# Order and queues of the first loads of a fused conditioning + low-rank FFN kernel, with a shorter warm-up and an earlier table load

## The reference, cut to what matters

```python
# x (64, 64, 1024) fp32; cond (64,) ints in 0..15; weights (16, 64, 64)
y = einsum('bct,bcd->bdt', x, weights[cond])          # conditioning, one 64x64 matrix per sample
yf = y.reshape(4096, 1024)
scores = yf @ Wr.T                                     # 64 experts
top_vals, top_idx = top_k(scores, 16)
G = zeros.at[rows, top_idx].set(softmax(top_vals))
h = einsum('nd,krd->nkr', yf, A)                       # A (64, 16, 1024): a 1024x1024 product
out = einsum('nkr,kdr->nd', h * G[:, :, None], B)      # B (64, 1024, 16): another one
return x + 2.0 * out
```

## Time and profile before

| | |
|---|---|
| runs (3) | 737.46 us median, 737.09 to 738.64 |
| the profiled execution | 737.22 us |
| its span, first to last instruction | 735.4 us |
| mean granted clock of PE | 0.995 of 2.4 GHz |
| PE busy | 716.5 us, 97% |
| PE weight loads busy | 600.9 us, 82% |
| DVE busy | 490.9 us, 67% |
| ACT busy | 262.8 us, 36% |
| POOL busy | 51.4 us, 7% |
| DMA | 178.41 MB, mean 243 GB/s |

### The profile page before, as it was taken

How to read it: one execution, slowest core, us unless ns; L and a number is a source line. 1 busy time by engine, 2 the same in 40 slices (tenths; PEclk the granted TensorE clock), 3 DMA queues, 4 the chain that set the end, 5 groups by cost and what they waited for, 6 DMA issues and landing times.

```text
span 735.4 us, 9259 instructions
## 1 busy us (share of the span) xinstructions
PE 716.5 (97%) x3440; PEld 600.9 (82%) x3440; DVE 490.9 (67%) x945; ACT 262.8 (36%) x498; POOL 51.4 (7%) x38
## 2 busy tenths in 40 slices
PE   8999989789999999999999999999999999999998
PEld 7878777578888888888888888888888888888886
DVE  4598899997433867965435469885544386887742
ACT  4567663332532642122222443312222264223100
POOL 0694700000000000000000000000000000000000
PEclk9999999899999999999999999999999999999999
DMA  9958349556986775566668586747577767544663
GB/s 321 408 202 289 121 166 404 210 209 261 310 309 227 285 261 203 210 215 235 238 245 289 200 324 236 246 162 270 199 256 256 270 249 290 185 170 175 228 227 143
DMA packets 56158, 178.41 MB, mean 243 GB/s; under 512 B 9650, under 2 KB 9778, under 8 KB 55602
## 3 DMA queue, kind: packets, MB, share of 16 engines
q1 hardware_dynamic: 53954, 172.78, 64.8%
q10 hardware_dynamic: 2160, 5.05, 1.9%
HBM read 131.66 MB, written 46.14 MB: 242 GB/s over the span
## 4 chain that ended last, share of the span: by engine, by line
PE 85%; DVE 13%; DMA 1%; issue 1%; ACT 0%; POOL 0%; DVEq 0%; POOLq 0%
PE Pb L265 38%; PE Pb L247 35%; PE Cb L227 6%; PE S L281 4%; DVE Cq L363 3%; DVE Wt L198 3%; DVE Op L180 2%; DMA xc<-in_x 1%; PE T L509 1%; DVE R L363 1%; DVE Xo L180 1%; DVE BR L363 1%; DVE xc L363 1%; DVE Q L363 1%; PE T L298 0%
## 5 line engine op out<-in xcount | busy, mean ns | idle before, releaser
L247 PE MATMUL Pb<-Op,Wt 128*128 128x512 f32 x1008 | 239.2, 393 | 6.4 <-DVE Op L180 4.6
L247 PEld LDWEIGHTS Pb<-Op,Wt 128*128 128x128 f32 x1008 | 187.4, 188 | 46.2 <-DVE Op L180 6.3
L265 PE MATMUL Pb<-Wt,Op 128*128 128x512 f32 x912 | 214.8, 394 | 7.0 <-DVE Op L180 7.0
L265 PEld LDWEIGHTS Pb<-Wt,Op 128*128 128x128 f32 x912 | 171.3, 190 | 43.5 <-DVE Op L180 8.7
L363 DVE TENSOR_TENSOR Q<-Pb,Q 128x512 f32<-128x512 f32 x112 | 77.4, 691 | 88.3 <-PE Pb L265 88.3
L265 PE MATMUL Pb<-Wt,Ox 128*128 128x512 f32 x432 | 100.8, 391 | 0.0
L265 PEld LDWEIGHTS Pb<-Wt,Ox 128*128 128x128 f32 x432 | 80.6, 188 | 16.3
L233 ACT COPY R<-Cb 128x512 f32<-128x512 f32 x60 | 35.2, 586 | 161.7 <-PE Cb L227 161.7
L180 DVE TENSOR_TENSOR Op<-R,Op 128x512 fp32r<-128x512 f32 x94 | 68.5, 753 | 28.8 <-ACT Op L178 28.8
L363 DVE TENSOR_TENSOR Cq<-Pb,Cq 128x512 f32<-128x512 f32 x64 | 44.0, 687 | 40.9 <-ACT Cq L374 30.9
L247 PE MATMUL Pb<-Ox,Wt 128*128 128x512 f32 x288 | 66.3, 390 | 0.0
(11 more groups left out here) (89 smaller groups left out, 486.9 us busy)
## 6 DMA issues: line engine op xcount, KB each, us to landing
Wt<-Wd SPq DMA_DIRECT2D x168, 512.0 KB, 4.9
Wd<-Wt SPq DMA_DIRECT2D x56, 512.0 KB, 4.2
Q<-in_x SPq DMA_DIRECT2D x32, 512.0 KB, 5.0
xc<-in_x SPq DMA_DIRECT2D x24, 512.0 KB, 4.0
out<-Q SPq DMA_DIRECT2D x32, 256.0 KB, 2.5
out<-Q SPq DMA_DIRECT2D x16, 512.0 KB, 2.8
BR<-in_x SPq DMA_DIRECT2D x12, 256.0 KB, 10.1
BR<-in_B SPq DMA_DIRECT2D x3, 1024.0 KB, 7.9
```

Source lines behind the costliest of these rows:

```text
L247: t = pe.run(lambda e, c=c, o=o, a=a, z=z: e.matmul(Pb[:, b, :], Wt[:, k, a, 128 * c:128 * c + 128], part(o, z), start=fresh and (c, a, z) ...
L265: t = pe.run(lambda e, c=c, o=o, k=k, a=a, z=z: e.matmul(Pb[:, b, :], part(o, a)[:, 128 * i:128 * i + 128], Wt[:, k, z, :], start=fresh an ...
```

## The change

- `WARM` goes from 24 to 14.
- The x blocks and A's half tiles that the first product uses are dealt to both queues: SP has x0, x1, x3 and A tiles 1 and 3; ACT has the table, x2, and A tiles 0 and 2. `Wr` and the identity come next on ACT, Wr now first.
- ACT does a 128x4 copy into `nm` behind its third issue, so that its table load stands there.
- A's tiles 4 to 7 move from the end of ACT's queue to the end of SP's.
- Unit 0 is split behind block 0, unit 1 behind block 2, unit 2 behind the first R copy; the second set of `wbd` copies (`cond_first(1)`) stands behind the R copies.
- The identity is awaited in `s_turn` and `g_turn` instead of before the loop.

```diff
-WARM = 24
+WARM = 14
@@ s_turn, g_turn
-            pe.after(tok, t_free[0])
+            pe.after(tok, t_free[0], t_id)
@@ the first loads
+        t_wa = ac.load(l_xc[0], lambda e: e.dma_start(Wa, wts))
         cn = sp.load(l_cn, lambda e: e.dma_start(cnd[:, :], cond.rearrange("(a b) -> a b", a=1)))
-        t_wa = ac.load(l_xc[0], lambda e: e.dma_start(Wa, wts))
-        for i in range(4):
-            load_x0(sp, i, 1)
-        for i in range(4):
-            load_an(ac, i, 1)
+        load_x0(sp, 0, 1)
+        load_x0(sp, 1, 1)
+        load_x0(ac, 2, 1)
+        load_x0(sp, 3, 1)
+        load_an(ac, 0, 1)
+        ac.after(z_s)
+        ac.run(lambda e: e.copy(nm[:, :], sS[:, 0:4]), False)
+        load_an(sp, 1, 1)
+        load_an(ac, 2, 1)
+        load_an(sp, 3, 1)
+        t_wr = ac.load(l_wr, lambda e: e.dma_start(SG[:, 0, :], Wr))
+        t_id = ac.load(l_id, lambda e: e.dma_start(idn[:, :], ident[:, :]))
         for i in range(4):
             load_x0(sp, i, 0)
-        t_id = ac.load(l_id, lambda e: e.dma_start(idn[:, :], ident[:, :]))
-        t_wr = ac.load(l_wr, lambda e: e.dma_start(SG[:, 0, :], Wr))
         for i in range(4):
             load_an(ac, i, 0)
         for a in range(2):
             for i in range(4, 8):
                 load_x0(sp, i, a)
         for j in range(4, 8):
-            load_an(ac, j, 0, 2)
+            load_an(sp, j, 0, 2)
@@ the four blocks
-            if i == 2:
-                a_unit(0, 0, an_ready[0][1])
+            if i == 0 or i == 2:
+                a_unit(0, i // 2, an_ready[i // 2][1])
         ops = [(op_spare.popleft(), parts[3]) for c in range(4)]
-        op_free[NO + 4] = cond_first(1)
         for i in range(4):
             ac.after(parts[i])
             R_ready[0][1] = ac.run(lambda e, i=i: e.copy(R[:, 0, 4:8, 128 * i:128 * i + 128],
                                                          banks[i].rearrange("p (c n) -> p c n", n=128)))
             (cb_free[0], cb_free[1], s_free, t_free)[i][0] = R_ready[0][1]
-            if i < 2:
-                a_unit(0, 1 + i, an_ready[1 + i][1])
+            if i == 0:
+                a_unit(0, 2, an_ready[2][1])
+        op_free[NO + 4] = cond_first(1)
         a_unit(0, 3, an_ready[3][1])
@@ before the main loop
-        pe.after(t_id)
```

## The result

Over 17 runs of each the changed kernel took 738.47 us (737.36 to 739.63), the kernel before 737.08 (735.89 to 738.83). The ratio is 1.0017, with a 95% interval of 1.0009 to 1.0024: **slower by 1.4 us**. That is just under the 1.5 us that the prediction took as the least that can be told from no change, but the interval leaves no change out. The forecast was 737.3, no change. The profiled executions stand at 738.47 and 737.22.

The account below looks back on a forecast made before the run. It took POOL's sums, in turns with VectorE, to set the T1 product, and PE to bound the next 22 us. 737.22 - 0.15 = 737.1, at the median's level 737.3; range 735.8 to 739.9.

Parts of the forecast that it names:

- The start: First product: would start at 13.0 instead of 14.79 us, a gain of 1.8 us there.
- Tile 4: Load of A's tile 4, at SP's end: lands at 24.3 to 25.3 us, 2.0 to 3.0 later than before.
- Gain at the T1 product: 0.15 us: Where PE resumes with T1: 54.3 instead of 54.45 by the sum of POOL and VectorE operations.
- the far bound: T1 product if tile 4 lands at 25.3: resumes at 55.3, a loss of 0.75 us.
- my 54.3: Forecast resumption of the T1 product: POOL's start at 24.3 plus 19.8 plus 10.2 us.
- the account: Up to T1: POOL's start plus tile waits, 18 POOL sums at 1.10 and 17 VectorE operations at 0.60 us.
- A, the account holds: Whole kernel: 737.3 us, own range 736.2 to 738.2; chance 0.50, together with the case that the start does not move.
- clock rival C: At the T1 wait: PE's clock falls, costing 2.0 to 3.4 us; 739.4, up to 740.7; chance 0.30.
- the 3 forecast: PE's wait before the T1 product: grows from 1.44 to some 3 us.
- The clock before the first product: Wait of about 2.1 us before the first product: clock could fall, largely swallowed by the T1 wait.
- Rival B, the gain survives: Whole kernel: turns do not set VectorE's time, 1.8 to 2.1 us moves on; 735.5; chance 0.20.
- turns: Before T1: POOL and VectorE operations on two SBUF inputs alternate, 1.10 us for POOL and 0.60 for VectorE.

Follow-up runs that it names:

- e4: The kernel before with only A's tiles 4 to 7 moved to the end of SP's queue: 738.76 us (12 runs), ratio 1.0017.
- e2: The changed kernel with 7 filler matmuls on zeros before the first product: 738.35 us (12 runs), ratio 1.002 to the kernel before.
- e1: The changed kernel with A's tiles 4 to 7 back at the end of ACT's queue: 734.57 us (9 runs), ratio 0.9966 to the kernel before.
- e5: The changed kernel with A's tiles 4 to 7 on ACT, 7 filler matmuls before the first product and 6 at T1: 733.95 us (5 runs).
- e8: The changed kernel with POOL's twelve sums for S3, S2 and S4 cut from 512 to 8 columns: 733.56 us (4 runs).
- e3: The changed kernel with 9 filler matmuls in the wait for the third piece of T1: 736.96 us (12 runs), ratio 0.9997 to the kernel before.
- e7: The changed kernel with A's tiles 4 to 7 back on ACT and WARM = 24: 735.87 us (9 runs), ratio 0.9975 to the kernel before.
- e10: The changed kernel with A's tiles 4 and 6 on ACT, 5 and 7 on SP ahead of x loads, no filler: 736.87 us (11 runs).
- e6: The kernel before with WARM = 14 alone: 737.14 us (11 runs), ratio 0.9995.

## Why the prediction was wrong

- **The start: right.** First product at 12.87 for 13.0; unit 1's cast stood ahead of the fourth block's (10.69 and 11.21), as taken. The table load behind the third issue (2.12 to 3.40, ACT's next issue at 2.18 beside it), the later weight copies (13.85) and the identity held up nothing that the trace shows.
- **Tile 4: right within its bounds,** 24.8 for 24.3 to 25.3, 2.4 us later than before.
- **"Gain at the T1 product: 0.15 us": the step that failed first.** It was a loss of 0.76, the far bound. I had taken the earliest landing, 24.3, where the bounds offered 25.3. Of the 1.0 us from my 54.3 to 55.31, 0.6 is that (POOL started at 24.87), and 0.4 is that the account runs short by 0.2 to 0.5 whenever POOL starts near 25 us. Its first four sums then have no waits, but three of them run beside VectorE's operations from 26.80 on, and the four take 5.95 us where they took 5.5 without their waits before.
- **"A, the account holds", as the likeliest: the second.** The mechanism held, but I gave the clock rival C 0.30, and it occurred. It was also overpriced: 1.45 us measured, not 2.0 to 3.4, because the low stretch held 3.1 busy us, half of which is 1.55, not 4.0 or more. (The sum had a slip beside that: 2.0 on 737.3 is 739.3, not 739.4.) The wait there was 2.41 us, not the 3 forecast, since the low clock of the first product had taken most of PE's lead. The sum 0.76 + 1.45 = 2.2 is what the trace shows up to 98 us. The rule of the Trainium skill (TensorE: Matmul & The Clock Gate, HAM oscillation), that work behind a long enough idle stretch starts cold, agrees with this trace in direction. It does not tell which waits are long enough here: 2.40 us at the T1 product of e4 left the clock up.
- **The clock before the first product.** I said that it could fall there and would be swallowed. It fell (1.49 us on the first product) and was swallowed: taking it away alone changed nothing (e2).
- **Rival B, the gain survives: wrong for this change.** The variant with the tiles on ACT gains 2.5 us, more than B's 1.8, but not by B's way, that turns do not set VectorE's time: they still do (20.57 + 2.0 + 30.0 for T1 at 52.58). I did not see that the tiles, left on ACT's queue, would let POOL start 1.9 us sooner than before.
- **Not foreseen:** about 0.9 us came back at the x load of 216 us. Over all profiles that wait is there in six of thirteen, 0.41 to 1.14 us: in four of five with the tiles on ACT, in one of six with them on SP, in one of two with them split. e1 and e5 have the same early schedule and differ in it, so the execution has a part in it, but the placing of the tiles may have one too. What decides it stays open. The medians' 1.4 us is therefore a mix of executions, not the ledger of one.

Shown by runs: the tile move is the loss (e1, e4), it works through the turns (e8, and the table), and the low clock after T1 is 1.5 us of the profiled loss (e3). In sum, the step that failed is the gain of 0.15 us at the T1 product, with the clock fall left at no cost in the forecast. The trace shows a loss of 0.76 us and another of 1.45 in its place; of the two, 0.9 came back later. Argued only: that the narrower spread of e5 is the clock's, and that the earlier first product is what e1 has over e7.

## What to carry to other kernels

When loads are reordered, ask for every transfer that moves back who waits for it, also off the critical path: here POOL's sums, by way of turns with VectorE, gave an early start back with interest. A shorter start is worth nothing while a second lane (the last tiles to POOL) sets the next meeting point, and a longer wait there can cost the clock on top. Test the parts of such a bundle alone: with one line undone this one was 2.5 us faster than the kernel before instead of 1.4 slower.

## What the runs showed of the hardware that I had not expected

- The same PE wait had different outcomes for the clock: after 1.80 us in e8 and 2.07 in e1 it stayed at 2.4 GHz, after 1.81 in the changed kernel it was at 1.2 GHz from 14.0 to 17.4, and it fell as well after 1.87 in e3, 1.97 in e10 and 2.23 in e6. At T1 it fell after 2.41, 3.51 and 3.09 us, and not after 1.44 or 1.48; but after 2.40 in e4 and 2.01 in e10 it did not, and after 1.92 in e7 it did. The wait that ends at 96.45 in the kernel before is 2.38 to 2.40 us long in all thirteen profiles; behind it the clock fell in four (the changed kernel, e3, e4, e8) and stayed in nine. A wait near 2 us is a matter of the execution.
- While POOL has sums in hand, a VectorE operation on two SBUF inputs takes 1.70 us instead of 0.63 to 0.69 (6.79 against 2.51 for four). The Trainium skill (GPSIMD Engine Reference, Key points) names the sharing; e8 shows its price here, about 4 us of VectorE's time in those four alone. An operation with one input in PSUM is not slowed: 0.68 us beside POOL's sums (Cq from Pb at 44.08 in the kernel before).
- A transfer at the end of a queue with its own engine's short list landed much sooner than one behind a long list, though the two queues share the engines (52.9% and 52.5% of them in the earlier trace rows): tile 4 at 20.5 on ACT in e1 against 24.8 on SP in the changed kernel, with the same bytes to be moved in all.
